# Turning three of every four routed tiles on VectorE, with their rows gathered eight tiles ahead

## What is computed

```python
logits = x @ gate_w.T                       # 2048 rows, 8 experts
probs = softmax(logits); w, sel = top_k(probs, 2); w = w / w.sum(-1)
out  = (silu(x @ shared_gate.T) * (x @ shared_up.T)) @ shared_down.T
for e in range(8):                           # each row goes to 2 of 8 experts, INNER = 352
    y[e] = (silu(x @ gate[e].T) * (x @ up[e].T)) @ down[e].T
out = out + sum over the row's two experts of w * y[e]
```

## Time and profile before

| | us |
|---|---|
| runs: median (lowest to highest) of 3 | 1554.25 (1554.23 to 1562.36) |
| profiled execution, its own time | 1556.24 |
| span of its instructions | 1554.5 |
| PE / DVE / ACT / POOL busy in the span | 1537.8 / 1156.4 / 581.8 / 453.6 |
| routed stage, first up matmul to last add | 1277.28 to 1542.27 |

### The profile page before, as it was taken

The page is one execution under the profiler, slowest core; times in us unless marked ns, Lnnn a source line. Parts: engine busy times, 40 slices in busy tenths (PEclk is TensorE's granted clock), DMA queues, the critical chain, the costliest instruction groups (busy, mean ns, idle before and its releaser), DMA issues.

```text
span 1554.5 us, 24017 instructions
## 1 busy us (share of the span) xinstructions
PE 1537.8 (99%) x7728; PEld 1324.3 (85%) x7729; DVE 1156.4 (74%) x2519; ACT 581.8 (37%) x997; POOL 453.6 (29%) x391
## 2 busy tenths in 40 slices
PE   8999999999999999999999999999999999999998
PEld 7888888888888888888888888888888889999897
DVE  4898887788887788886787778745663677877774
ACT  4454443434444334444344344333112223333332
POOL 4445432234222233222233221113210013433341
PEclk9999999999999999999999999999999999999999
DMA  8886764677886686985686878376440256778644
GB/s 311 286 302 234 232 219 144 239 293 266 303 297 224 245 317 234 322 311 202 252 309 245 325 277 320 105 234 192 133 151 27 80 207 214 211 235 258 183 88 81
DMA packets 106838, 353.94 MB, mean 228 GB/s; under 512 B 11312, under 2 KB 31792, under 8 KB 101232
## 3 DMA queue, kind: packets, MB, share of 16 engines
q1 hardware_dynamic: 93520, 314.62, 55.8%
q0 software_dynamic: 13216, 38.02, 10.3%
HBM read 228.34 MB, written 124.26 MB: 227 GB/s over the span
## 4 chain that ended last, share of the span: by engine, by line
PE 80%; DMA 11%; DVE 4%; issue 2%; POOL 1%; ACT 1%; SPq 1%; POOLq 0%; DVEq 0%; ACTq 0%
PE bank L385 26%; PE bank L387 26%; PE bank L386 26%; DMA out<-x_early,ids_e 9%; PE bank L2041 1%; DMA rows<-x_rows,ids_e 1%; DMA wqk_raw<-wqk_in 1%; DMA wqk<-wqk_parts 1%; SPq L398 0%; DMA wv_raw<-wv_in 0%; POOL wqk L707 0%; POOL store L707 0%; PE bank L2162 0%; DVE resid L1518 0%; DVE place_hot L1694 0%
## 5 line engine op out<-in xcount | busy, mean ns | idle before, releaser
L751 POOL TENSOR_TENSOR probs<-probs,causal 128x256 f32<-128x256 f32 x126 | 90.4, 738 | 401.9 <-ACT probs L931 401.9
L387 PE MATMUL bank<-store,wqk 128*128 128x512 f32 x512 | 199.9, 390 | 0.0
L385 PE MATMUL bank<-store,wqk 128*128 128x512 f32 x512 | 199.7, 390 | 0.2 <-DMA wqk<-wqk_parts 0.2
L386 PE MATMUL bank<-store,wqk 128*128 128x512 f32 x512 | 199.8, 390 | 0.0
L1322 DVE SCALAR_TENSOR_TENSOR resid<-bank,factor,resid 128x512 f32<-128x512 f32 x256 | 189.4, 741 | 1.3 <-PE bank L387 1.2
L707 POOL TENSOR_TENSOR pre_split<-pre_raw,pre_split 128x1536 fp32r<-128x1536 f32 x34 | 119.4, 3513 | 141.7 <-ACT pre_split L893 141.7
L929 ACT ACTIVATE probs<-bank 128x512 f32<-128x512 f32 x189 | 85.8, 528 | 131.4 <-PE bank L387 131.4
L1529 DVE STREAM_TRANSPOSE bank<-rows 32x128 f32<-32x128 f32 x288 | 120.2, 417 | 7.6 <-DMA rows<-x_rows,ids_e 2.8
L1316 DVE TENSOR_TENSOR q_lo<-bank,q_hi 128x512 fp32r<-128x512 f32 x64 | 44.3, 691 | 93.5 <-ACT q_hi L976 93.4
L387 PEld LDWEIGHTS bank<-store,wqk 128*128 128x128 f32 x512 | 96.1, 188 | 20.3
L385 PEld LDWEIGHTS bank<-store,wqk 128*128 128x128 f32 x512 | 96.2, 188 | 18.7 <-DMA wqk<-wqk_parts 0.6
(11 more groups left out here) (355 smaller groups left out, 3980.2 us busy)
## 6 DMA issues: line engine op xcount, KB each, us to landing
pre_parts<-pre_split SPq DMA_DIRECT2D x34, 1536.0 KB, 6.6
wqk<-wqk_parts SPq DMA_DIRECT2D x96, 512.0 KB, 4.1
pre_raw<-pre SPq DMA_DIRECT2D x34, 768.0 KB, 8.1
store<-wv_parts SPq DMA_DIRECT2D x12, 2048.0 KB, 9.5
wo<-wo_parts SPq DMA_DIRECT2D x48, 512.0 KB, 7.3
expert_w<-pre_parts SPq DMA_DIRECT2D x8, 2816.0 KB, 11.6
wqk_parts<-wqk SPq DMA_DIRECT2D x16, 1024.0 KB, 5.2
expert_w<-pre_parts SPq DMA_DIRECT2D x8, 1536.0 KB
```

The lines of the kernel that those rows point to most:

```text
L385: nc.tensor.matmul(out_ap, a_hi, b_hi, start=first, stop=False)
L386: nc.tensor.matmul(out_ap, a_hi, b_lo, start=False, stop=False)
L387: return nc.tensor.matmul(out_ap, a_lo, b_hi, start=False, stop=last)
L751: nc.gpsimd.tensor_tensor(diagonal, diagonal, causal[:, :, :], ALU.mult).then_inc(S["masked"], 1)
```

## The change

- Tiles 6 to 38 whose number leaves another remainder than 1 on division by four are turned by DVE, 25 tiles where it was 18; even ones into bank 6, odd ones into bank 3. PE turns tiles 0 to 5 and 9, 13, ... 37, 14 where it was 21.
- The order of the channels on the partitions is changed: both kinds of turn now read contiguous channels (32 a run for DVE, 128 for PE). The host lays out the experts' gate and up weights to match; no work moves on the chip for that.
- Three more row buffers, `more_rows`. Tiles with remainder 0, 2 or 3 have two buffers in turn and are gathered in POOL's step g - 8; tiles with remainder 1 keep one buffer, and step g - 6.
- The parts of DVE's turns are spread so that each step of DVE has 12 block turns, 4 in its middle and 8 at its end.
- Two more steps of PE's loop are written out.

```diff
-        XT_DVE = 6
+        XT_DVE = (6, 3)
+        DEEP = (0, 2, 3)
+        more_rows = sb("more_rows", [P, len(DEEP), D])
...
-        E_ROWS, E_AHEAD = 4, 6
+        E_ROWS = 4
+        def row_depth(g):
+            return 2 * E_ROWS if g % E_ROWS in DEEP else E_ROWS
+        def gathered_after(g):
+            return g - (8 if g % E_ROWS in DEEP else 6)
+        def rows_e(g):
+            at = g % E_ROWS
+            return rows[:, at, :] if g % row_depth(g) < E_ROWS else more_rows[:, DEEP.index(at), :]
+        FIRST_DVE = 6
         def by_dve(g):
-            return g >= E_ROWS and g % 2 == 0
+            return g >= FIRST_DVE and g % 4 != 1
...
-                if g >= E_ROWS:
-                    pool.wait_ge(S["e_xT_ready"], g - E_ROWS + 1)
-                nc.gpsimd.indirect_dma_start(rows[:, g % E_ROWS, :], ...
+                if g >= row_depth(g):
+                    pool.wait_ge(S["e_xT_ready"], g - row_depth(g) + 1)
+                nc.gpsimd.indirect_dma_start(rows_e(g), ...
...
-            for g in range(E_AHEAD):
-                gather(g)
+            for g in range(ETILES):
+                if gathered_after(g) < 0:
+                    gather(g)
             pool.wait_ge(S["stored"], 16 * (LATE_AT + 1))
             for g in range(ETILES):
-                if g + E_AHEAD < ETILES:
-                    gather(g + E_AHEAD)
+                for t in range(g, ETILES):
+                    if gathered_after(t) == g:
+                        gather(t)
                 add_rows(g)
...
-                    part = rows[i * BLOCK:(i + 1) * BLOCK, t % E_ROWS, q * P:(q + 1) * P].rearrange("p (y k) -> p k y", k=KC)
+                    part = rows_e(t)[i * BLOCK:(i + 1) * BLOCK, :].rearrange("p (k n) -> p k n", k=KC)[:, :, q * BLOCK:(q + 1) * BLOCK]
...
+                early, late = (
+                    ([(g + 2, 3 * n // 4, n)], [(g + 3, 0, n // 2)]),
...
-                    last = nc.tensor.transpose(bank[XT][:, k * P:k * P + P], every(rows[:, j % 4, :], k), ident[:, :])
+                    last = nc.tensor.transpose(bank[XT][:, k * P:k * P + P], row[:, k * P:k * P + P], ident[:, :])
```

More of the change, by code:

```diff
@@ L350, in build @@
         SH_PIECES = 2 * (2 * KC + 4)
-        E_ROWS, E_AHEAD = 4, 6
+        E_ROWS = 4
[7 more added lines that the diff above has]
+        FIRST_DVE = 6
         def by_dve(g):
-            return g >= E_ROWS and g % 2 == 0
+            return g >= FIRST_DVE and g % 4 != 1
         def xT_bank(ph, g):
-            of = XT_DVE if ph == "e" and by_dve(g) else XT
+            of = XT_DVE[g % 2] if ph == "e" and by_dve(g) else XT
             return bank[of][:, :].rearrange("p (k n) -> p k n", k=KC)
@@ L839, in gather @@
                     pool.wait_ge(S[f"e_row{g % 2}"], 16 * (g // 2))
-                if g >= E_ROWS:
-                    pool.wait_ge(S["e_xT_ready"], g - E_ROWS + 1)
-                nc.gpsimd.indirect_dma_start(rows[:, g % E_ROWS, :], None, x3_rows, bass.IndirectOffsetOnAxis(ids_e[:, g:g + 1], 0)).then_inc(S[f"e_row{g % 2}"], 16)
+                if g >= row_depth(g):
+                    pool.wait_ge(S["e_xT_ready"], g - row_depth(g) + 1)
+                nc.gpsimd.indirect_dma_start(rows_e(g), None, x3_rows, bass.IndirectOffsetOnAxis(ids_e[:, g:g + 1], 0)).then_inc(S[f"e_row{g % 2}"], 16)
             def add_rows(g):
@@ L1790, in _, with turns_at, turn_rows_e @@
             xT_low("e", 0)
-            for g in range(ETILES - 1):
[L1792 to L1797, removed]
+            def turns_at(g):
+                n = QUADS * QUADS
+                early, late = (
+                    ([(g + 2, 3 * n // 4, n)], [(g + 3, 0, n // 2)]),
+                    ([(g + 2, n // 2, 3 * n // 4)], [(g + 2, 3 * n // 4, n), (g + 3, 0, n // 4)]),
+                    ([(g + 2, n // 4, n // 2)], [(g + 2, n // 2, n)]),
+                    ([(g + 3, 0, n // 4)], [(g + 3, n // 4, 3 * n // 4)]))[g % 4]
+                return [[part for part in parts if FIRST_DVE <= part[0] < ETILES] for parts in (early, late)]
+            def turn_rows_e(parts):
+                for part in parts:
+                    turn_row_parts_e(*part)
+            for g in range(ETILES - 1):
+                early, late = turns_at(g)
+                step("e", g, first=g == 0, between=lambda: turn_rows_e(early))
+                turn_rows_e(late)
             step("e", ETILES - 1, last=True, between=lambda: aT_low_s(LATE_AT))
@@ L2160, in transpose_rows_e @@
                 pe.wait_ge(S[f"e_row{j % 2}"], 32 * i + 16 * (j // 2) + 16)
+                row = rows_e(E_ROWS * i + j) if isinstance(i, int) else rows[:, j % E_ROWS, :]
                 for k in range(KC):
-                    last = nc.tensor.transpose(bank[XT][:, k * P:k * P + P], every(rows[:, j % 4, :], k), ident[:, :])
+                    last = nc.tensor.transpose(bank[XT][:, k * P:k * P + P], row[:, k * P:k * P + P], ident[:, :])
                 last.then_inc(S["e_xT_ready"], 1)
@@ L2173, in e_step @@
                     p = place(g - 1)
-                    if early or not by_dve(E_ROWS + j + 1):
+                    if early or not by_dve(2 * E_ROWS + j + 1):
                         transpose_rows_e(i, j + 1)
@@ L2209, in _ @@
             e_step(0, 1, second=False, early=True)
-            by_fours(pe, e_step, 2, ETILES - 2)
+            e_step(0, 2, early=True)
+            e_step(0, 3, early=True)
+            by_fours(pe, e_step, 4, ETILES - 2)
             last = ETILES - 1
@@ L2255 @@
         "pre": c(np.concatenate([flat(m.T) for m in f(ctx_2048)] + [flat(sh_up), flat(chunks(sh_down))]
-                                 + [m for wu, wd in zip(up, down) for m in (flat(wu), flat(chunks(wd)))] + [np.zeros((P, PRE_COLS - EXP_AT - EXPERTS * (UP + DOWN)), np.float32)], 1)),
+                                 + [m for wu, wd in zip(up, down) for m in (flat(chunks(wu)), flat(chunks(wd)))] + [np.zeros((P, PRE_COLS - EXP_AT - EXPERTS * (UP + DOWN)), np.float32)], 1)),
     }
```

## The result

The changed kernel takes 1567.05 us, the median of 8 runs (1564.7 to 1570.33); the kernel before, run beside it, 1556.7 (8 runs, 1554.23 to 1562.36). The ratio is 1.0063, 95% interval 1.0049 to 1.0077: 9.8 us slower by the ratio. The forecast was 1567.2, or 12.9 us slower. That the first median comes within 0.2 us of it is luck: the kernel before was taken as 1554.25 and came out at 1556.7, and the change cost less than forecast by about as much.

A forecast was written before the change was run, and what follows sets the result against it. The prediction took the routed stage's serial adds to `out` as the bound, PE close second. POOL's queue +14.0 us and PE's turns -1.1 us gave +12.9, from 1554.25 to 1567.2 us; 8-in-10 range 1559 to 1577.

The forecast's parts named there:

- The sum: Whole kernel: 14.0 us for POOL's queue less 1.1 us for PE's turns, +12.9 us, a median of 1567.2 us.
- 2.0 us a double step: POOL issues two gathers in one step, the second waiting for the first to land; add interval 7.5 us, 2.0 more.
- Seven times, low 0, high +8 for one that meets a load: POOL's steps 3, 7, ... 27 with two gathers: +14.0 us, low 0, high 22, with 8 more at a weight load.
- PE's turns, -1.1 us: PE saves 5.3 us of its own time; only the last add's wait for PE counts, -1.1 us.
- DVE, 290 ns a block: DVE's contiguous block turns take 290 ns; four tiles take 22.3 of PE's 25.5 us, so no cost.
- Initial gathers, 0: Eight instead of six gathers ahead of the first add: delay absorbed by step 3, zero; at most 3 us.
- Product buffers off the path: With four product buffers ACT waits for adds and PE stands still 5 to 15 us, at no cost in time.
- Second gather hardly waits: On POOL, two gathers in a step cost 0.8 us or less: +4.5 us, 1558.8 us; chance 0.15.
- PE sets the end: The adds' chain shortens enough that the last add follows PE: 3.3 + 2.0 us come off, 1549.0 us; chance 0.04.
- DVE as the bound: DVE's turns stay at 417 ns, tiles take 7.1 us, last add 19 us later: 1573 us; chance 0.11.
- Double steps that meet loads: Two of POOL's seven two-gather steps meet a weight load alone, costing 8 us instead of 2: +12, 1579 us; chance 0.08.

The follow-up runs named there:

- eight buffers: Changed kernel with ACT's copy waiting for the add eight tiles before, not four: 1574.19 us, 1.0095 of before; again 1574.62 us, 1.0092.
- strided reads: Changed kernel with DVE and PE turns reading every fourth channel again and the old weight layout: 1578.64 us, 1.0116 of before.
- six-ahead version: Changed kernel with every tile gathered six ahead into four buffers, as before the change: 1557.12 us, 0.9984 of before.
- pieces two at a time: Changed kernel, all gathers six ahead, each part of an expert's weights loaded in four pieces, two on their way: 1551.92 us, 0.9951 of before.
- small loads: Most weights of experts 2 to 7 left unloaded: kernel before 1553.13 us (0.9954 of before), changed kernel 1551.75 us (0.9948).

## Why the prediction was right, point by point

- **The sum.** +12.9 us was forecast; +9.8 and +13 were measured in two sets of runs. In the stage itself, from the first gather to the last add, the two traces of the changed kernel have 8.7 and 17.0 us more than the one of before. The interval between adds as the unit, and the queue of POOL as the place, hold: moving one gather in four by one step takes the cost away, and adding the wait alone to the kernel before brings +7 or +20 us.
- **2.0 us a double step.** In quiet stretches 1.8 to 2.6 in the two traces, mean 2.2. The wait for the first gather, 3.55 us behind its 1.01 of issue, is the 3.8 to landing and 0.7 on the row. The rule of the Trainium skill ("DMA: Bandwidth & Descriptors", the anatomy of a GpSimd DMA), 2.6 us for 256 KB as an estimate, would have left 2.6 - 1.0 + 0.7 = 2.3 us between the two issues at the most; the trace has 3.55, so it doesn't agree here.
- **"Seven times, low 0, high +8 for one that meets a load."** Right in the bounds; the even price is borne out for the four quiet steps alone. Step 3 met a load: 15.29 us, after which the adds stood 5.5 us, nearly one whole add, later than before (add of tile 4 at 57.28 against 51.83 us from the first gather), and so within 0.5 us in the traces with eight buffers and strided reads; in the second trace of the changed kernel it is 8.0. Steps 7 and 11 met loads too, and in the first trace the rest of the loads gave all of it back: the three come to -0.4 us together. In the second they come to 6.1, just the 3 x 2.0 of the forecast. Why executions of one kernel differ by that much is open. What a load costs the adds lies between 3.4 and 8.9 us in the five traces in which I read it load by load (before, after, one gather later, six ahead, eight buffers), with the same bytes, and with no order that I could find. The text treated a load as a fixed price; that 7 x 2.0 comes near the total rests in part on luck, since the draw of the loads moves an execution by as much as the three steps were to cost.
- **PE's turns, -1.1 us.** Right in principle: PE's gain can't be had while the adds set the end. Mis-sized: the six-ahead version has -2.5 (0 to -5), and without whole loads the whole path is 6.4 us shorter. The 1.1 was read from one execution, which was shorter than 45 of the 51 runs beside the experiments.
- **DVE, 290 ns a block.** 323. In four tiles 48 x 0.336 + 7.9 = 24.0 us, still under PE's 25.5, so the term stays 0; at 417 it would be 28.5, and in the strided version PE's last product does come 19.6 us later. The nearest row (285 ns, a sum with a far smaller write) was too low, as the text feared.
- **Initial gathers, 0.** The add of tile 0 goes out 1.8 us later after the first gather (23.88 against 22.06), that of tile 2 0.2 us later. Right.
- **Product buffers off the path.** Right: ACT waited 22.8 us in 11 copies, PE stood still 4.5 us from 1370 to 1470 (2.1 before; 5 to 15 was forecast), and eight buffers gain nothing.
- **The rivals.** Second gather hardly waits: excluded by 3.55 us. PE sets the end: excluded by the lag of 9.1 us; with pieces two at a time it is just what happens, in another kernel. DVE as the bound: excluded by 323 ns a block; the strided version has its late products, but the adds are last even there. Double steps that meet loads: they did, three of seven, at 15.29, 9.89 and 12.52 us, but in the sum of the stage they cost -0.4 and 6.1 us, not three times 8.

## What to carry to other kernels

Where one engine issues serial transfers that set the end, count what stands in its queue between two of them: a prefetch that is early and harmless costs a landing each time it waits for another prefetch on a counted semaphore. Spread prefetches evenly, one between two of the serial transfers, or give those that stand together different semaphores (in the run with one gather in four a step later the second waits 0.30 us). And ask first what stretches the serial transfers themselves: here the shift of work between engines gave 2.5 us (0 to 5) without its prefetch, and cutting the weight loads some 5 more. Pieces in the kernel before, without the shift, were not run.

## What the runs showed of the hardware

- A 32x128 float32 block transpose on DVE takes 323 ns reading runs and 417 reading every fourth word; 94 ns for 128 elements a partition, 0.7 ns an element.
- An accumulating 256 KB DMA takes 4.5 to 4.8 us with no weights on their way. While 2816 and then 1536 KB of weights are on their way whole, the longest interval between adds at each load is 10.1 to 11.9 us before (8.8 at the least in the other traces with whole loads); with the same bytes in quarters, two at a time, none is over 8.4, at a DMA share of 0.88 and 0.89 in 1370 to 1420 and 1420 to 1470, where the same kernel with whole loads had 0.81 and 0.76. So the share of the DMA engines' time alone doesn't explain what holds an add. The Trainium skill ("DMA: Bandwidth & Descriptors", queues, rings and completion order) says that a DMA engine takes turns between queues packet by packet; whether the shorter rows of a piece (its runs are a quarter as long) or the fewer of them queued make the difference was not separated, and no run here tries one without the other.
- 19 runs of the kernel before spread over 10 us, 4 with small loads over 1.5 us: most of the spread seems to come with the loads. One profiled execution is a draw from it, and a slack of 1 us read there says little.
